# A cross-attention and expert kernel: two reorders of hand-ordered queues, in the first batch and in the last

## What is computed

```python
x = x + tanh(g_xattn) * attention(layernorm(x), ctx, Wq, Wkv, Wout)   # 4 batches x 512 x 512, 16 heads, 64 keys, causal
x = x + tanh(g_ffn) * ffn(layernorm(x))
# ffn:
scores = softmax(xf @ gate_w.T)                 # 2048 tokens, 8 experts
weights, idx = top_k(scores, 2)
y = sum over the two experts e of a token: weight * (silu(xf @ w1[e].T) * (xf @ w3[e].T)) @ w2[e].T
z = (silu(xf @ ws1.T) * (xf @ ws3.T)) @ ws2.T   # a shared expert, inner width 256
```

## Times and profile before

| | us |
|---|---|
| median of 3 runs | 464.53 (464.41 to 466.38) |
| the profiled execution | 467.39 |
| its span, first to last instruction | 465.7 |
| mean granted clock of PE over the span | 0.970 |

### The profile page before, as it was taken

One profiled execution on the slowest core, in us unless ns is written; L12 is line 12 of the kernel. 1 busy time (PEld: TensorE's weight loads), 2 busy tenths in 40 slices (PEclk: granted clock), 3 DMA queues, 4 the chain that ended last, 5 costly groups with the idle time before them and its releaser, 6 DMA issues.

```text
span 465.7 us, 8278 instructions
## 1 busy us (share of the span) xinstructions
PE 409.3 (88%) x2739; PEld 221.6 (48%) x2740; DVE 306.2 (66%) x663; ACT 239.5 (51%) x432; POOL 228.1 (49%) x205
## 2 busy tenths in 40 slices
PE   1877887999999999898868889989999999999980
PEld 1454443555545554464433345445555555555540
DVE  4977998789588876898839659954444444444430
ACT  2786875676647766756214136834443434344330
POOL 4008434537266762589350212755556565565422
PEclk9988998999999999999979899999999999999996
DMA  8930002606006076176168477966567666566553
GB/s 303 419 104 2 0 1 68 227 2 223 4 1 227 2 288 134 41 262 192 59 59 155 138 272 225 158 116 109 118 98 131 128 100 130 94 132 108 96 67 45
DMA packets 20768, 58.64 MB, mean 126 GB/s; under 512 B 3521, under 2 KB 3777, under 8 KB 20354
## 3 DMA queue, kind: packets, MB, share of 16 engines
q1 hardware_dynamic: 11234, 37.77, 25.9%
q0 software_dynamic: 9504, 20.48, 24.5%
HBM read 35.54 MB, written 22.70 MB: 125 GB/s over the span
## 4 chain that ended last, share of the span: by engine, by line
PE 54%; DVE 17%; POOL 8%; issue 8%; DMA 5%; ACT 5%; POOLq 1%; SPq 0%; DVEq 0%; ACTq 0%
PE bank L1664 40%; PE bank L1669 9%; DVE arena L1057 4%; ACT arena L701 3%; DMA lists<-pair,slot 2%; DVE mv L1093 2%; POOL lists L573 2%; POOL arena L588 2%; PE bank L1817 2%; PE bank L1806 2%; PE bank L1794 2%; POOL GT L613 2%; DVE mx L1178 1%; POOL ln L555 1%; DMA listed<-lists 1%
## 5 line engine op out<-in xcount | busy, mean ns | idle before, releaser
L1664 PE MATMUL bank<-arena,GT 128*128 x468 | 107.4, 379 | 2.8 <-issue 2.8
L685 POOL DMA_INDIRECT out<-rows,entry x39 | 61.8, 1586 | 72.1 <-issue 31.3
L1664 PE MATMUL bank<-arena,gT 128*128 (+1 forms) x336 | 80.2, 376 | 1.4 <-ACT rows L1032 1.0
L1664 PEld LDWEIGHTS bank<-arena,GT 128*128 128x128 f16 x468 | 45.8, 98 | 49.7 <-issue 3.5
L701 ACT ACTIVATE arena<-bank 128x512 f16<-128x512 f32 (+1 forms) x88 | 48.7, 587 | 26.1 <-PE bank L1664 12.0
L662 POOL DMA_INDIRECT rows<-xrows,entry x39 | 38.9, 997 | 43.4 <-DVE entry L1455 18.2
L1057 DVE SCALAR_TENSOR_TENSOR arena<-bank,arena 128x512 f16<-128x512 f32 (+1 forms) x72 | 44.7, 667 | 11.5 <-ACT arena L701 9.0
L1664 PEld LDWEIGHTS bank<-arena,gT 128*128 128x128 f16 x336 | 32.7, 98 | 37.6 <-issue 2.5
L1664 PE MATMUL bank<-arena,x2T 128*128 128x512 f16 x192 | 47.7, 400 | 2.1 <-DVE x2T L1056 1.7
L1056 DVE TENSOR_TENSOR gT<-bank,gT 128x256 f16<-128x256 f32 x55 | 23.0, 420 | 38.8 <-ACT gT L701 38.7
L1623 DVE SCALAR_TENSOR_TENSOR uu<-th,bank 128x256 f32<-128x256 f32 x39 | 16.4, 421 | 48.5 <-ACT th L999 46.8
(11 more groups left out here) (174 smaller groups left out, 648.3 us busy)
## 6 DMA issues: line engine op xcount, KB each, us to landing
x_sb<-in_experts SPq DMA_DIRECT2D x9, 768.0 KB, 4.7
rows<-in_experts SPq DMA_DIRECT2D x6, 768.0 KB, 6.2
xrows<-xn SPq DMA_DIRECT2D x16, 256.0 KB, 6.2
out<-x_sb SPq DMA_DIRECT2D x16, 256.0 KB
image<-GT SPq DMA_DIRECT2D x5, 768.0 KB, 4.2
arena<-image SPq DMA_DIRECT2D x10, 384.0 KB
x_sb<-in_x SPq DMA_DIRECT2D x1, 2048.0 KB, 15.5
x_sb<-in_x SPq DMA_DIRECT2D x2, 512.0 KB, 4.2
```

What stands on the lines that cost most here:

```text
L685: nc.gpsimd.indirect_dma_start(out=out, out_offset=bass.IndirectOffsetOnAxis(ap=entry[:, 1, j:j + 1], axis=0), in_=Y[:, j % RING, :], in_o ...
L1664: last = nc.tensor.matmul(dst, a, b, start=n == 0, stop=n == len(steps) - 1)
```

## The change

It moves instructions and a few waits, and adds one aggregate and one power. In the first batch: the first norm works in two groups of two tiles; `own_block` moves from there to behind the maxima; ACT does the third projection's high half ahead of `fill_k(0)` and the first `exps` ahead of the last scores; DVE does the sums one place earlier, and takes the statistics of tiles 12 to 15 all behind the last probabilities instead of between them; ACT does half of the shared expert's weights ahead of the scores' copy; DVE does x1 and its statistics ahead of the maxima. In the last batch: the low halves of x2 tiles 0 and 1 come ahead of the aggregate and of the placing; the scatters of the second choice wait for the last batch's logits; `turn_g(f - 1, ...)` and `base` take other places; `hidden(f, 3)` and `down(f - 1, 3)` stand ahead of `place_lists`; SP reads `listed` ahead of piece 11 and loads piece 12 ahead of the base stores, and gives its mark `landed` at its start; the low halves 14 and 15 are done ahead of the loop, so that `LO_FIRST` is 8 and the tables of ACT shift by one half; `down(B - 1, 3)` and its base move behind the first expert product.

The diff, cut to its core:

```diff
@@ -357,13 +357,13 @@
-        LN1_GROUPS = ((0, PER), (PER, 2 * PER), (2 * PER, NT))
+        LN1_GROUPS = ((0, 2), (2, PER), (PER, 2 * PER), (2 * PER, NT))
...
         PARTS = 4
-        HI_AT_TURN = {1: (20, 21), 2: (22, 23), 3: (24, 25), 4: (27, 28), 5: (30, 31)}
-        HI_AT_END = {3: (26,), 4: (29,)}
-        LO_FIRST = 7
+        HI_AT_TURN = {1: (20, 21), 2: (22, 23), 3: (25, 26), 4: (28, 29), 5: (31,)}
+        HI_AT_END = {2: (24,), 3: (27,), 4: (30,)}
+        LO_FIRST = 8
@@ -449,6 +449,7 @@
+sp.sem_inc(landed, 1)
@@ -484,23 +485,21 @@
 load_piece(9)
-sp.wait_ge(st_rows, 16 * NT)
-sp.wait_ge(turned, turn_no(B, "x2", PER - 1)[0])
-load_piece(11)
...
              lists[:, :].rearrange("(p f) c -> p (f c)", p=P)).then_inc(ld_listed, 16)
+sp.wait_ge(st_rows, 16 * NT)
+sp.wait_ge(turned, turn_no(B, "x2", PER - 1)[0])
+load_piece(11)
+sp.wait_ge(h_mm, NT)
+load_piece(12)
...
 load_piece(10)
-sp.wait_ge(h_mm, NT)
-load_piece(12)
...
     load_piece(k)
-sp.sem_inc(landed, 1)
@@ -562,6 +561,7 @@
 power1(0)
+power1(1)
@@ -623,7 +623,7 @@
     if prev is None:
-        power1(2)
+        power1(3)
@@ -646,9 +646,11 @@
     power2(b, 1)
-    scatter_pairs(prev)
-
-power1(1)
+    scatter_pairs(prev, (0,))
+    pool.wait_ge(lg_out, B)
+    scatter_pairs(prev, (1,))
+
+power1(2)
@@ -808,6 +810,8 @@
+
+def got0_high():
@@ -880,17 +884,16 @@
     turn_hi(c, "x2", 3)
+    turn_hi(f, "g", 2)
+    turn_hi(f, "g", 3)
...
     tanh_h(f, 1)
-    turn_hi(f, "g", 2)
-    turn_hi(f, "g", 3)
+    tanh_h(f, 2)
     send_lists()
-    tanh_h(f, 2)
-    turn_hi(c, "g", 0)
-    turn_hi(c, "g", 1)
     tanh_h(f, 3)
-    turn_hi(c, "g", 2)
-    turn_hi(c, "g", 3)
+    got0_high()
+    for i in range(PER):
+        turn_hi(c, "g", i)
@@ -899,16 +902,17 @@
     if prev is None:
+        exps(b, 0)
         scores_out(b, 3)
-        exps(b, 0)
         exps(b, 1)
+        exps(b, 2)
...
             project_hi(b + 1, n)
-            if prev is None and n < 2:
-                exps(b, n + 2)
+            if prev is None and n == 0:
+                exps(b, 3)
@@ -926,9 +930,9 @@
         hi(aTv[:, 0, g, :], mm_bank[g][:, :], S_A / (S_P * S_KV)).then_inc(a_hi, 1)
-    scores_out(b + 1, 0)
...
         shared_hi_half(1)
+    scores_out(b + 1, 0)
@@ -966,8 +970,8 @@
 act.wait_ge(k_lo, NG)
+project_hi(0, 2)
 fill_k(0)
-project_hi(0, 2)
@@ -1083,8 +1087,8 @@
-    dve.wait_ge(ln1_power, 1)
     for i in range(PER):
+        dve.wait_ge(ln1_power, 1 + i // 2)
@@ -1147,12 +1151,10 @@
-dve.wait_ge(ld_x0[0], 16)
-statistics1(range(2))
-dve.wait_ge(ld_x0[1], 16)
-statistics1(range(2, PER))
-aggregate1(0)
-own_block()
+for n in range(2):
+    dve.wait_ge(ld_x0[n], 16)
+    statistics1(range(2 * n, 2 * n + 2))
+    aggregate1(n)
@@ -1350,7 +1352,9 @@
     x1_and_statistics(b, 3)
+    turn_lo(b + 1, "x2", 0)
     aggregate2(b, 1)
+    turn_lo(b + 1, "x2", 1)
@@ -1478,22 +1482,21 @@
     c = f + 1
-    turn_lo(c, "x2", 0)
-    turn_lo(c, "x2", 1)
     norm2(f, 1)
+    base(f - 1, 0)
...
     turn_lo(c, "x2", 3)
-    base(f - 1, 0)
+    turn_lo(f, "g", 2)
+    turn_lo(f, "g", 3)
...
     last_place(f)
-    turn_lo(f, "g", 2)
-    turn_lo(f, "g", 3)
+    hidden(f, 1)
+    base(f - 1, 1)
     rows_hot()
-    hidden(f, 1)
@@ -1501,17 +1504,18 @@
     read_table()
-    base(f - 1, 1)
     base(f - 1, 2)
+    hidden(f, 2)
     turn_lo(c, "g", 1)
-    hidden(f, 2)
     read_weights()
+    split_half(2 * LO_FIRST - 2)
+    split_half(2 * LO_FIRST - 1)
     base(f - 1, 3)
+    turn_lo(c, "g", 2)
...
     base(f, 0)
-    turn_lo(c, "g", 2)
+    turn_lo(c, "g", 3)
     base(f, 1)
-    turn_lo(c, "g", 3)
@@ -1530,8 +1534,10 @@
     if prev is None:
+        head_sum(b, 0)
         head_max(b, 3)
-        head_sum(b, 0)
+        head_sum(b, 1)
+        statistics1(range(11, 12))
@@ -1540,19 +1546,16 @@
             if prev is None and n < 2:
-                head_sum(b, n + 1)
+                head_sum(b, n + 2)
...
             values_lo(n)
-            if n == 0:
-                head_sum(b, 3)
...
                 head_sum(b, 3)
-            if prev is None:
-                statistics1(((11, 12), (13,), (14,), (15,))[n])
     if prev is None:
-        aggregate1(2)
+        statistics1(range(12, NT))
+        aggregate1(3)
@@ -1562,13 +1565,18 @@
            gate_s[:, 0].rearrange("p c e -> p (c e)"), S_W).then_inc(gate_lo, 1)
-    head_max(b + 1, 0)
-    x1_and_statistics(b, 0)
-    if prev is None:
-        bias1(2)
-    head_max(b + 1, 1)
-    x1_and_statistics(b, 1)
-    aggregate2(b, 0)
+        x1_and_statistics(b, 0)
+        head_max(b + 1, 0)
+        bias1(3)
+        x1_and_statistics(b, 1)
+        aggregate2(b, 0)
+        head_max(b + 1, 1)
+    else:
+        head_max(b + 1, 0)
+        x1_and_statistics(b, 0)
+        head_max(b + 1, 1)
+        x1_and_statistics(b, 1)
+        aggregate2(b, 0)
@@ -1586,9 +1594,9 @@
 statistics1(range(PER + 2, 2 * PER))
-aggregate1(1)
+aggregate1(2)
 project_lo(0, 1)
-bias1(1)
+bias1(2)
@@ -1596,17 +1604,19 @@
 V.tensor_scalar(gl[:, 1:2], gl[:, 3:4], 1.0 / (S_G * S_W), None, ALU.mult).then_inc(gates_ready, 1)
+project_lo(0, 3)
+turn_lo(0, "x", 0)
+turn_lo(0, "x", 1)
...
 statistics1(range(8, 10))
-project_lo(0, 3)
-turn_lo(0, "x", 0)
-turn_lo(0, "x", 1)
-statistics1(range(10, 11))
...
 turn_lo(0, "x", 3)
-for i in range(3):
-    head_max(0, i)
+head_max(0, 0)
+head_max(0, 1)
+statistics1(range(10, 11))
+head_max(0, 2)
+own_block()
@@ -1637,14 +1647,14 @@
         hidden_e(j + 1, (s + 1) % RING)
-    if isinstance(j, int) and j < LO_STEPS:
+    if isinstance(j, int) and j < LO_STEPS - 1:
...
 rows_lo(0, 0)
-base(B - 1, 3)
...
 hidden_e(0, 0)
+base(B - 1, 3)
@@ -1895,23 +1905,23 @@
     router(0, 2)
+    turn_g(f - 1, 2)
+    turn_g(f - 1, 3)
...
     hidden(f, 1)
-    turn_g(f - 1, 2)
-    turn_g(f - 1, 3)
...
     down(f - 1, 2)
+    hidden(f, 3)
+    down(f - 1, 3)
...
     turn_g(f, 1)
-    hidden(f, 3)
-    down(f - 1, 3)
+    down(f, 0)
     turn_g(f, 2)
-    down(f, 0)
@@ -2040,11 +2050,11 @@
 pe.wait_ge(table_ready, 2)
+e = expert_of(0)
 turn_rows(0, 0, 0)
+turn_rows(1, 1, 0)
+hidden_e(0, 0, e)
 down(B - 1, 3)
-turn_rows(1, 1, 0)
-e = expert_of(0)
-hidden_e(0, 0, e)
```

## The result

| | before | changed |
|---|---|---|
| median, us | 466.55 (20 runs, 464.12 to 470.72) | 463.78 (20 runs, 458.86 to 467.8) |
| ratio | | 0.991 (0.9887 to 0.9933) |
| profiled execution, us | 467.39 (span 465.7) | 466.09 (span 464.3) |

The change saves 0.9%, 4.2 us (3.1 to 5.3), where 7.6 was forecast; the 463.78 lies above the range's end of 462.5. The three runs from which I took 464.53 were at the low end of what the kernel before does: 2.0 us of the absolute miss is that. The rest is a gain that didn't come.

What follows compares the result with a forecast made beforehand. PE sets the end, the expert loop at its own pace; gains lie ahead of it and in its first steps. First batch -1.7, last batch -3.4, into the loop +0.4, first steps -2.96: -7.6, to 456.9 us; range 453.0 to 462.5.

Steps and rivals of the forecast that it cites:

- (a): First norm, first batch: two groups of two tiles start PE 1.0 us earlier; moving own_block costs nothing.
- (b): Projections, first batch: fill_k moved behind the third copy brings first scores 2.4 us earlier; 1.8 us carried on.
- (c): Mixing stage, first batch: statistics moved behind the last turn start attend about 2.7 us earlier; projection out keeps about 2.
- (d): x1 ahead of the head maxima, first batch: PE's turn 1.7 us earlier, but the clock's loss of 1.7 us stays.
- (e) to (i): Last batch, turns of x2 to the last down before the loop: -3.4 us, ends -5.1 and +1.7.
- (f): Router, last batch: its matmuls run without issue gaps, logits 4.7 us earlier; the other end is nothing.
- (h): Lists, last batch: load let go 5.2 us behind the last scatter, lists added at 255.9 instead of 258.46.
- rival of the late list: Last batch: lists still come 10.3 us behind the last scatter; sum -2.6, 461.9 us; chance 0.15.
- the slower one: Last batch: PE's issue gaps come with any four scatters beside stores, listed there at 264; 467 us; chance 0.05.
- (j): Into the loop: down(B-1, 3) and its base behind the first expert product cost +0.4 us, ends -0.5 and +1.0.
- (k): The loop's first steps: the waits of three late products all go, -2.96 us, at least -2.2.
- the first batch gives nothing: First batch: moved statistics delay DVE's copies by all that attend won; 458.6 us; chance 0.11.

Runs made afterwards that it cites:

- first_only: The kernel before with the reorder of the first batch alone; ratio 1.0038 to the kernel before, 1.8 us slower.
- after: The changed kernel in its first profiled execution, 466.09 us; its timed runs have a median of 463.78 us, ratio 0.991.
- again: The changed kernel, unchanged, run once more for a second trace; ratio 0.9908 to the kernel before.
- first_free: The kernel before with the first batch's reorder alone and own_block ahead of the fourth projection's low half; ratio 0.999.
- own_free: The changed kernel with own_block ahead of the low half of the fourth projection, where POOL is idle; ratio 0.9836 to the kernel before.
- own_down: own_free with down(B-1, 3) and its base between the two turns of rows, low halves 14 and 15 behind the second turn's low half; ratio 0.9778.
- no_second: The changed kernel without the last four scatters of batch 2, the load of the lists not waiting for them; ratio 0.9777.
- halves_back: own_free with low halves 14 and 15 back in the loop's first step and the tables of the kernel before; ratio 0.9857.
- own_free2: own_free repeated on another chip; ratio 0.986 to the kernel before.
- late_mark: The changed kernel with SP's mark landed moved back behind SP's last load; ratio 0.9909 to the kernel before.
- last_only: The kernel before with the reorder of the last batch alone, mark and weight halves with it; ratio 0.9883, 5.5 us faster.
- eight: The changed kernel with the eight scatters in one piece, without the wait for the logits; ratio 0.9986 to the kernel before.

## Why the prediction was wrong

**(a)** The first turn came at 8.65 (8.8 forecast).

**(a), last sentence: the step that failed.** "The three small instructions of own_block move behind the score maxima, where DVE waited for ACT; nothing." I priced them by their rows ahead of the first norm, 0.15 to 0.22 us, and looked at DVE's wait that would hide them, not at what POOL does at the new place. There a POOL operation of 1.9 us is running, and the instructions last until it ends: 2.5 us more of DVE in first_only, 1.6 in after. What PE loses by it is 2.5 us where its scores ran fast and 0.4 where they ran slow, as in after and again. By the ratios it is 2.3 us (first_only to first_free), 3.4 and 1.6 (changed kernel to own_free), each with an interval of 2 us or more either way. So of the miss of 3.4 it is a part that changes with the execution, the larger one only in those with a fast PE.

**(b), "I carry 1.8 on": the other step.** The product behind the scores is where this gain has to be. It stands at 39.6 to 39.8 in the three traces of the old order. In the fifteen of the new one it stands at 37.8 to 38.2 six times, which is the forecast, at 40.2 to 40.4 three times and at 41.4 to 41.7 six times; the mean is 39.9. In the late ones PE is for the most part at the lower of its two clock levels behind the first scores (granted clock of 33.0 to 41.5 in the kernel before, after and own_down; columns as in the earlier trace rows):

```profile
33.00:41.50 8.50, 6.15 (x81) 4.08 (x80) 5.56 (x6) 5.31 (x11) 6.26 (x4) 0.70 0.01 2
```

```profile
33.00:41.50 8.50, 6.04 (x81) 4.84 (x82) 7.48 (x12) 5.14 (x11) 5.13 (x4) 0.54 0.00 1
```

```profile
33.00:41.50 8.50, 6.15 (x92) 3.64 (x90) 8.20 (x11) 6.14 (x11) 6.42 (x4) 1.00 0.02 5
```

I had allowed for the clock only at the turn of x2. Its fall in the scores takes back the 1.8 us, and in the latest six as much again.

The first scores, forecast at 28.4, are at 28.26 in no_second, whose first products ran as fast as in the kernel before (first turn to first context product 10.95 us). In after, where they ran slow, they are at 31.00.

**(c)** Right in its mechanism, wrong in its sum. PE's waits ahead of attend shrink from 3.6 to 2.4 us (1.3, 0.6 and 1.7 before; 0.6, 0.3 and 1.5 after), not by 2.7: most of the statistics had stood inside waits of DVE for ACT. And they do cost their full 2.5 us ahead of the four copies. Attend at 58.6, the sign that I had named, is met where PE's scores ran fast and own_block is out of the way (58.66 in own_down, 58.75 in halves_back, 58.98 in own_free2). Behind it the move of the statistics takes back 1.1 us net, by every trace of either kind. The times of whole runs are too coarse for this: 0.974 and 0.9779 against own_down's 0.9778, and 0.9932 (0.997 with all times) against first_free's 0.999.

**(d)** The turn of x2 comes 1.3 us sooner behind attend than in the kernel before once the statistics are out of the way (15.0 against 16.3). The forecast had it at 75.9, all gains counted; own_down, halves_back and own_free2 have it at 75.3 to 75.5, the other twelve at 76.5 to 79.5. From the first values product to this turn the changed order brings 1.0 us, where the forecast brought in 1.8 and took out 1.7; what is missing at the turn had been lost before. The clock's loss there "stays", I said: from this turn to the next one the way takes 3.1 us in after, again and first_only, and 4.6, 4.8 and 5.9 in own_free2, late_mark and last_only (4.7 in the kernel before). Either order shows both, so that it goes by the execution. There is a cost that I had not seen: a small TENSOR_SCALAR of the second aggregate now meets POOL as well, and PE waits 0.66 us for the next turn:

```profile
83.19 0.75 DVE L1106 TENSOR_SCALAR ln<-ln 128x2 f32<-128x2 f32 x1
...
85.35 0.66 PE L1675 MATMUL bank<-ident,xn 128*128 128x128 f32 x4 [0.66 <-DVE xn L1149]
```

(first_only; the TENSOR_SCALAR takes 0.17 us in the kernel before.)

**(e) to (i)** From the turn of x2 in the last batch to the first turn of rows: 42.1 us in the mean of five traces of the old order (41.2 to 43.1), 37.8 in the mean of seven of the new one (36.4 to 40.9): -4.3, with -3.4 forecast and ends of -5.1 and +1.7. Within it (f), 4.7 us at the logits, measured 4.0 to 5.4. (h) was optimistic: the lists were let go 5.9 us behind the last scatter in after and 7.3 in again, where 5.2 was taken, and the second four start only when DVE has the logits. But the landing was short, 

```profile
254.90 0.32 SPq L490 DMA_DIRECT2D listed<-lists  x1
...
257.01 0.23 DVE L1441 CAST got<-listed 128x128 f16<-128x128 int32 x1 [2.28 <-DMA listed<-lists]
```

2.1 us (again) instead of 5.1. The last weight load ahead of it in SP's queue is 13.9 us old there, and was 4.8 us old in the kernel before. The two errors cancel. The rival of the late list (10.3 us) did not happen, though own_free came near with 9.5; nor did the slower one.

**(j)** 8.68 us from the first turn of rows to the second product, 8.26 before (7.95 to 8.35 in the five traces of the old order): +0.4 to +0.5, as forecast.

**(k)** 185.5 to 185.8 us from the second product to the end, 188.6 to 189.4 with the old order: -3.3 in the means, -2.96 forecast. The two waits for halves are the halves' (halves_back); that the third needed the mark is wrong (late_mark).

So of the forecast's -7.6, -5.9 was for the last batch and the loop and measured -5.5 by last_only's ratio (-7.1 by the means of the traces), and -1.7 for the first batch and measured +1.8. With own_block repaired the ratio is 0.984 to 0.986, 6.6 to 7.7 us, which is near what I had forecast for the whole; but part of that is luck, since the first batch by itself (first_free) stays 1.2 us short of its forecast and the two halves run apart make 6.0. The rival "the first batch gives nothing" named (c) rightly as the weak term, but no rival had the first batch slower, since I had put a nought for own_block without a row of it beside POOL's operations of 1.9 us.

**Open.** What makes PE's scores slow in nine of fifteen traces with the new order. From the first turn to the product behind the scores it takes 29.7, 29.7 and 30.0 us in the three traces with the old order, and in fifteen with the new one 29.0 to 29.5 six times, 31.4 to 31.7 three times and 32.7 to 32.8 six times. That an earlier first norm, or the new order of the scores, brings this about is a rival that no run here tests: three traces of the old order can't tell, and none of the experiments takes that part of the change back by itself. Nor can I say what holds the handover to DVE back behind the scatters (4.98 us in eight, 3.19 once in after).
